# A routed mixture of experts: other queues, places and order for the loads of its sums, and an earlier read of the ring place

## The reference, cut to what matters

```python
router_scores = jax.nn.sigmoid(t @ Wr)
_, idx = jax.lax.top_k(router_scores + expert_bias[None, :], TOPK)
w = jnp.take_along_axis(router_scores, idx, axis=1)
w = w / jnp.sum(w, axis=-1, keepdims=True)
wfull = jnp.zeros((T, E), jnp.float32).at[jnp.arange(T)[:, None], idx].set(w)
g = jnp.einsum('th,ehi->tei', t, Wg)
u = jnp.einsum('th,ehi->tei', t, Wu)
act = jax.nn.silu(g) * u
moe = jnp.einsum('tei,te,eih->th', act, wfull, Wd)
shared = jax.nn.silu(t @ Wsg) * (t @ Wsu) @ Wsd
return resid + (moe + shared).reshape(B, S, H)
```

## Time and profile before

| what | value |
|---|---|
| median of 3 runs | 2467.36 us (2466.81 to 2470.5) |
| the profiled execution | 2468.82 us, span 2467.0 us |
| mean granted TensorE clock | 0.954 |
| PE busy | 2212.2 us, 90% |
| DVE busy | 1313.1 us, 53% |
| ACT busy | 927.0 us, 38% |
| POOL busy | 986.5 us, 40% |
| DMA | 194.38 MB, mean 79 GB/s |

### The profile page before, as it was taken

How to read it: one execution, slowest core, us unless ns; L and a number is a source line. 1 busy time by engine, 2 the same in 40 slices (tenths; PEclk the granted TensorE clock), 3 DMA queues, 4 the chain that set the end, 5 groups by cost and what they waited for, 6 DMA issues and landing times. The chain is left out here.

```text
span 2467.0 us, 41046 instructions
## 1 busy us (share of the span) xinstructions
PE 2212.2 (90%) x15152; PEld 1594.1 (65%) x15152; DVE 1313.1 (53%) x2358; ACT 927.0 (38%) x1630; POOL 986.5 (40%) x787
## 2 busy tenths in 40 slices
PE   7889999688999998889999998578879999979998
PEld 7658776577888887543333333166657777759997
DVE  4563666647777777533333332485762666653333
ACT  1332222344454553245655555013543323232221
POOL 2334544555656563225656564153433101012220
PEclk9999999799999999989999999788999999979999
DMA  3011100221111110657666868630011000011110
GB/s 122 24 58 49 39 27 1 73 82 56 53 60 51 61 43 1 232 169 183 128 127 166 230 163 274 136 88 25 2 55 58 26 26 26 1 52 52 51 51 30
DMA packets 56910, 194.38 MB, mean 79 GB/s; under 512 B 8261, under 2 KB 8517, under 8 KB 49861
## 3 DMA queue, kind: packets, MB, share of 16 engines
q1 hardware_dynamic: 39444, 152.95, 18.6%
q0 software_dynamic: 17280, 38.94, 8.2%
HBM read 158.70 MB, written 33.16 MB: 78 GB/s over the span
## 5 line engine op out<-in xcount | busy, mean ns | idle before, releaser
L2095 PE MATMUL bank<-m_ring,m_bT 128*64 x576 | 265.1, 603 | 22.2 <-issue 13.0
L2097 PE MATMUL bank<-m_upper,m_bT 128*64 128x512 f32 x576 | 265.4, 604 | 0.0
L2008 DVE SCALAR_TENSOR_TENSOR m_prod<-bank,m_slot_rows,m_silu 64x256 f32<-64x256 f32 x144 | 69.6, 483 | 293.5 <-ACT m_silu L1768 291.7
L2095 PEld LDWEIGHTS bank<-m_ring,m_bT 128*64 128x64 f32 x576 | 73.6, 138 | 162.8 <-issue 162.8
L1739 POOL DMA_INDIRECT m_sum<-m_yb,m_idx x72 | 102.8, 1428 | 168.9 <-DVE m_yb L2019 161.1
L1823 ACT ACTIVATE m_upper<-m_ring 128x1024 f32 x144 | 143.5, 1046 | 1.4 <-issue 1.2
L856 ACT ACTIVATE y_att_p_rows<-bank,y_att_n_top 112x375 f32<-112x375 f32 x128 | 71.7, 573 | 189.6 <-DVE y_att_n_top L898 189.6
L2124 PE MATMUL bank<-m_ring,m_aT 128*64 x288 | 135.4, 592 | 0.8 <-DVE m_aT L2025 0.8
L2126 PE MATMUL bank<-m_upper,m_aT 128*64 128x512 f32 x288 | 135.4, 592 | 0.0
L225 PE MATMUL bank<-f_hT_hi,f_w_hi 128*128 128x448 f32 x288 | 109.3, 380 | 9.1 <-PEq L91 2.7
L1283 POOL TENSOR_TENSOR f_att_turned<-f_att_turned,consts 128x448 f32<-128x448 f32 x64 | 74.8, 1170 | 102.7 <-ACT f_att_turned L1333 102.7
(11 more groups left out here) (498 smaller groups left out, 6204.2 us busy)
## 6 DMA issues: line engine op xcount, KB each, us to landing
m_ring<-in_m_w SPq DMA_DIRECT2D x32, 1536.0 KB, 7.7
f_raw<-in_f_wq SPq DMA_DIRECT2D x64, 256.0 KB, 2.6
z_raw<-in_z_w SPq DMA_DIRECT2D x7, 1536.0 KB, 6.4
f_att_wo_raw<-in_f_wo SPq DMA_DIRECT2D x16, 512.0 KB, 3.7
m_sum<-m_slot_rows SPq DMA_DIRECT2D x4, 2048.0 KB, 18.2
x_c_raw<-in_ctxT SPq DMA_DIRECT2D x8, 752.0 KB, 4.3
y_c_raw<-in_ctxT SPq DMA_DIRECT2D x8, 752.0 KB, 4.2
a_raw<-in_a_wqk SPq DMA_DIRECT2D x8, 256.0 KB, 2.6
```

Of the source, the lines that this page charges most:

```text
L2095: pe.matmul(ps_gu[u % 2][0:HP, :], bT[:, n % 2, k, 0:HP], ring[:, bass.ds(slot + at, D)], start=(k == 0), stop=(k == KC - 1))
L2097: o = pe.matmul(ps_gu[u % 2][HP:P, :], bT[:, n % 2, k, HP:P], upper[:, n % 2, at:at + D], start=(k == 0), stop=(k == KC - 1))
```

## The change

Four things are done. SP's loop over the odd sums goes; ACT issues these two loads (`load_odd`), behind its work for block 64 (NBLK - TAIL + 2), and the loads no longer wait for the ring. `add_odd` runs behind the last three blocks, three sequences behind block 69, three behind 70, two behind 71. For the last sums SP issues the four loads of sum 0 into `y`, each with a semaphore of its own, and ACT issues the four of sum 1 into `x2`, between the silu and the copy of shared unit 6; DVE takes the products of units 5, 6 and 7 and the sum of unit 5 ahead of the adds. And PE reads the rank of block n + 1 and works out its place and its count for the ring between the gate products of block n and the down products of block n - 1.

```diff
--- before.py
+++ after.py
@@ -1643,7 +1643,7 @@
 
         (consts_in, wr_in, shared_in, ring_in, rows_set, tail_set, share_set, sums_set) = map(sem, (
             "consts_in", "wr_in", "shared_in", "ring_in", "rows_set", "tail_set", "share_set", "sums_set"))
-        early_in = sem("early_in")
+        early_in = [sem(f"early_in{h}") for h in range(B // 2)]
         late_in = [sem(f"late_in{h}") for h in range(B // 2)]
         rows_in = [sem(f"rows_in{i}") for i in range(NR)]
         summed = [sem(f"summed{i}") for i in range(4)]
@@ -1671,6 +1671,13 @@
         def pairs_in(at, n):
 
             return sum(sums_of(m) == at for m in range(n))
+
+        def load_even(e, i, into, arrived):
+            e.wait_ge(summed[i], 16 * pairs_in(0, NBLK))
+            for h in range(B // 2):
+                e.dma_start(into[:, 2 * h:2 * h + 2, :],
+                            sums_dram[i][2 * h * S:2 * (h + 1) * S, :].rearrange("(b s) d -> s b d", b=2)
+                            ).then_inc(arrived[h], 16)
 
         def unit_of(b):
 
@@ -1707,18 +1714,8 @@
                     sp.wait_ge(dn_done, last + FRONT)
                 sp.dma_start(ring[:, bass.ds(at, EW)], w_dram[bass.ds(expert, 1)].squeeze(0)).then_inc(ring_in, 16)
             sp.wait_ge(ring_in, 16 * E_MOE)
-            for i, into in ((2, y), (3, x2)):
-                sp.wait_ge(summed[i], 16 * pairs_in(i // 2, NBLK))
-                sp.wait_ge(x_done, B)
-                sp.dma_start(into[:, :, :], sums_dram[i][0:T, :].rearrange("(b s) d -> s b d", b=B)).then_inc(odd_in, 16)
-            for i, into in ((0, y), (1, x2)):
-                sp.wait_ge(summed[i], 16 * pairs_in(0, NBLK))
-                if i == 0:
-                    sp.wait_ge(odd_done, B)
-                for h in range(B // 2):
-                    sp.dma_start(into[:, 2 * h:2 * h + 2, :],
-                                 sums_dram[i][2 * h * S:2 * (h + 1) * S, :].rearrange("(b s) d -> s b d", b=2)
-                                 ).then_inc(late_in[h] if i == 1 else early_in, 16)
+            sp.wait_ge(odd_done, B)
+            load_even(sp, 0, y, [early_in[h] for h in range(B // 2)])
 
         @block.gpsimd
         def _(pool):
@@ -1829,6 +1826,12 @@
                 act.activation(upper[:, n % 2, 2 * KC * EI:EW], ring[:, bass.ds(slot + 2 * KC * EI, NC * D)],
                                ACT.Copy).then_inc(upper_done, 1)
 
+            def load_odd():
+                act.wait_ge(x_done, B)
+                for i, into in ((2, y), (3, x2)):
+                    act.wait_ge(summed[i], 16 * pairs_in(1, NBLK))
+                    act.dma_start(into[:, :, :], sums_dram[i][0:T, :].rearrange("(b s) d -> s b d", b=B)).then_inc(odd_in, 16)
+
             collect_rows(0)
             collect_rows(1)
             act.wait_ge(tabs_done, 4)
@@ -1845,9 +1848,16 @@
                     copy_upper_down(n + 1, slot)
                 if n + 2 < NBLK:
                     collect_rows(n + 2)
-            for b in range(FRONT, B):
-                silu_of(unit_of(b))
-                collect_a(unit_of(b))
+                if n == NBLK - TAIL + 2:
+                    load_odd()
+            silu_of(unit_of(FRONT))
+            collect_a(unit_of(FRONT))
+            silu_of(unit_of(FRONT + 1))
+            act.wait_ge(odd_done, B)
+            load_even(act, 1, x2, late_in)
+            collect_a(unit_of(FRONT + 1))
+            silu_of(unit_of(FRONT + 2))
+            collect_a(unit_of(FRONT + 2))
 
         @block.vector
         def _(dve):
@@ -2039,12 +2049,12 @@
                 if n:
                     collect_y(n - 1)
                 collect_block(n)
-                if n >= NBLK - 4:
-                    for b in range(2 * (n - NBLK + 4), 2 * (n - NBLK + 4) + 2):
+                if n >= NBLK - 3:
+                    for b in range(3 * (n - NBLK + 3), min(3 * (n - NBLK + 3) + 3, B)):
                         add_odd(b)
             def add_first(b):
                 dve.wait_ge(add_done, b + 1)
-                dve.wait_ge(odd_done, b + 1)
+                dve.wait_ge(early_in[b // 2], 16)
                 dve.tensor_tensor(x[:, b, :], x[:, b, :], y[:, b, :], ALU.add).then_inc(first_sum, 1)
 
             def add_last(b):
@@ -2056,24 +2066,19 @@
 
             collect_y(NBLK - 1)
             prod_shared(5)
-            dve.wait_ge(early_in, 16 * (B // 2))
-            for b in range(FRONT):
+            prod_shared(6)
+            add_shared(5)
+            prod_shared(7)
+            for b in range(6):
                 add_first(b)
-            add_shared(5)
-            prod_shared(6)
-            add_first(5)
-            for b in range(3):
+            add_shared(6)
+            for b in range(4):
                 add_last(b)
-            prod_shared(7)
-            add_last(3)
-            add_shared(6)
+            add_shared(7)
             add_first(6)
-            add_last(4)
-            add_last(5)
-            add_shared(7)
             add_first(7)
-            add_last(6)
-            add_last(7)
+            for b in range(4, B):
+                add_last(b)
 
         @block.tensor
         def _(pe):
@@ -2224,18 +2229,23 @@
             pe.wait_ge(etab_done, 1)
             turn_rows(0)
             turn_rows(1)
+            def slot_of(n):
+                rank = pe.value_load(rtab[0:1, 2 * n:2 * n + 1], min_val=0, max_val=E_MOE - 1)
+                return pe.snap(rank % RING * EW), pe.snap(rank * 16 + 16)
+
+            slot, loaded = slot_of(0)
             for n in range(NBLK):
-                rank_now = pe.value_load(rtab[0:1, 2 * n:2 * n + 1], min_val=0, max_val=E_MOE - 1)
-                slot = pe.snap(rank_now % RING * EW)
-                pe.wait_ge(ring_in, rank_now * 16 + 16)
+                pe.wait_ge(ring_in, loaded)
                 pe.wait_ge(bT_done, n + 1)
                 gate_up_halves(n, slot)
+                if n + 1 < NBLK:
+                    slot_next, loaded = slot_of(n + 1)
                 if n:
                     down_halves(n - 1, slot_before)
                 if n + 2 < NBLK:
                     turn_rows(n + 2)
                 turn_a(FRONT + n)
-                slot_before = slot
+                slot_before, slot = slot, slot_next
             down_halves(NBLK - 1, slot_before)
             shared_up(FRONT)
             for b in range(FRONT, B):
```

## The result

The changed kernel takes 2428.15 us (median of 4 runs, 2420.88 to 2430.01) against 2468.93 us for the kernel before beside it (4 runs, 2466.81 to 2473.66): a ratio of 0.9825, 95% interval 0.9805 to 0.9845. That is faster, clear of no change though by less than 2%, and 2429.0 was forecast. Its profiled execution took 2430.01 us, with a span of 2428.2 us (before 2467.0). The total came out right, but two terms of its sum did not, and they nearly cancel.

A forecast was written before the change was run, and what follows sets the result against it. PE bound the late loop, with a 26.6 us wait for DVE, itself held by late odd loads. Stage end 1534.3 + 40.1 + 0.3 = 1574.7 against 1612.96: 38.3 us less, so 2429.0 us, range 2414 to 2444.

The forecast's parts named there:

- Part 1: PE's joint between blocks: reading the ring place earlier gains 0.3 us a block, 18 us up to gate 61.
- Rival B: PE's joint keeps its length, since a change of product form costs what the read did: 2448 us, chance 0.12.
- Rival C: PE's register read waits until queued gate products are done, 1.0 us more a block: 2518 us, chance 0.03.
- Part 2: Late loop: ACT issues odd loads early, adds from block 69; a 12 us stall replaces the 27, gate 71 at 1534.3.
- whatever POOL issues meanwhile lands behind them: Late loop: gathers and scatters issued after the odd loads wait for them, a new stall of 12 us.
- they land at about 1499: Late loop: the odd loads, 3.6 MB, take 14 us of all DMA engines after the ring load landing at 1485.
- a 12 us stall in front of gate 67: PE wants block 68's gather at 1492.4, but it lands at 1504 to 1504.5.
- Rival A: Late loop: odd loads do not block the gathers, so the 12 us stall goes: 2417 us, chance 0.2.
- Three adds a block: DVE's late-loop odd adds: six operations, 4.1 us, make the next product 0.4 us late; 0.3 charged once.
- a sign of being wrong: Gather after the odd loads landing within 5 us, blocks staying at 6.4 us, or DVE waiting for pieces behind the loop.
- Part 3: Behind the loop: DVE makes products before adds, ending 40.1 us behind gate 71; gain 2.1 us, second queue 0.2 of issue.

The follow-up runs named there:

- e7: The changed kernel with PE's read of the ring rank and its arithmetic done four times in a row instead of once; 2430.42 us, ratio 0.9839.
- e1: The kernel before with only PE's register read moved behind the gate products; 2444.91 us, ratio 0.9891.
- e4: The changed kernel with 21 ring loads in place of 32, leaving out ranks 21 to 31 that no block reads; 2421.47 us, ratio 0.9804.
- e6: The changed kernel with two odd adds behind each of blocks 68 to 71, as before the change; 2424.03 us, ratio 0.9814.
- e10: The changed kernel with ring loads ended behind the last rank in use and two odd adds behind each of blocks 68 to 71; 2415.12 us, ratio 0.9797.
- e12: The changed kernel itself, same text, run once more; 2429.49 us, ratio 0.9845.
- e9: The changed kernel with SP's ring loads ended behind the last rank that a block reads, by a count from the rank table; 2415.94 us, ratio 0.9791.
- e3: The changed kernel with both last sums issued by SP and DVE's adds in the order of before; 2431.94 us, ratio 0.9835.
- e5: The changed kernel with SP issuing all eight pieces of the last sums and ACT none, DVE's new order kept; 2428.16 us, ratio 0.9844.

## Why the prediction was right, step by step

| term | forecast | profiled execution | off by |
|---|---|---|---|
| gate 1 to gate 61 against before | -18.2 | -19.1 | -0.9 |
| gates 61 to 71 | 77.8 (-18.2) | 73.56 (-22.5) | -4.2 |
| gate 71 to the end | 40.4 (-1.8) | 42.65 (+0.4) | +2.2 |
| gate 1, unchanged code | 0 | +2.6 | +2.6 |
| end of the stage | -38.3 | -38.5 | -0.2 |

The forecast puts gate 61 at 1456.5, though its own 18 us from 1474.7 make 1456.7; the table keeps what it used.

**Part 1 was right, in mechanism and size.** Blocks of 6.11 us, no idle time at the gates, 0.32 us a block against 0.3. The switch from transposes to gate products costs what was taken: the last transpose starts 0.20 us before the gate, 0.11 us between transposes. The read is at the gate (0.1 us behind it, not 0.5), earlier than said. Rival B (the joint keeps its length) and Rival C (the read waits for queued products) fall with this and with e7.

**Part 2: the step that failed** is "whatever POOL issues meanwhile lands behind them", with "they land at about 1499" beside it. The loads were issued when I said (1482.88, forecast 1481.8), but landed at 1503.1 and 1517.6. I had given them all DMA engines for 14 us; they share them with the ring loads, three of which took 10.1, 12.9 and 9.2 us where 7.7 was the step before. And small transfers were not held until the odd loads were in: they landed 0.7 us ahead of to 3.4 us behind the ring load in flight, near what the earlier trace rows had. The gather for block 68, for which I forecast a 12 us stall in front of gate 67, was in time. The stall was 6.5 us, in front of gate 69, with 1.3 and 0.7 before it: 8.5 in place of 12 and the pace of landings behind it. By e1, ring loads at the pace of part 1 make 7.1 us of such waits without any odd load, a cost that the forecast did not have by itself. Rival A, by which the odd loads hold nothing back, was nearer for e4's first scatter, but it charged nothing, and the runs lie between: such a transfer takes 3.6 us alone, 7.2 to 8.9 just behind a ring load, 6.9 and 8.4 beside the odd loads (e4), and up to 11.5 beside both. The Trainium skill (DMA: Bandwidth & Descriptors, Queues, rings and completion order) says that each DMA engine goes round between its queues, packet by packet. The trace agrees in that the scatter of 1482.93 landed 12.7 us before an odd load issued ahead of it, and not in that slipping in would be free.

I had also left out what the clock adds to a stall. PE was busy for 1.49 us of the 8 from 1508 to 1516; from 1516 to 1519 it worked without a pause at a granted clock of 0.50 (1.2 GHz), and from 1522 on at 1.00 (2.4 GHz), as the windows above show. At the half clock the pairs of gate products start 0.85 us apart and not 0.43, and gate 69 to gate 70 took 8.47 us, 2.4 over the usual.

Three adds a block made the product of block 70 late: PE waited 1.1 us for it, and gate 71 came 6.91 us behind gate 70, against 5.74 with two adds (e6, e10; block 70 turns no rows, so it is shorter than 6.11). That is 1.2 us where 0.3 was charged. The other two of PE's three waits for products lie behind gate 71.

The size of this term is not known as closely as the table looks: e12 has 79.05 for the same stretch, and 77.8 lies between the two. What failed is how it comes about, more than its sum.

**Part 3: DVE's order did what was forecast, but the pieces came later.** The forecast put the first piece of sum 0 at 14.45 us behind gate 71, as before; it was at 18.02. That is the second step that failed: each lower scatter waits for the landing of the last one, the ring loads held that chain until 1536.4, which is now 4.7 us behind gate 71, and gate 71 had moved ahead of the chain. Where the unused loads are gone the piece leaves at 14.80 to 15.59 (e10, e9, e4), which bears this out. The 3.6 us cost the end only part of themselves, since product 7 comes no sooner: DVE's six first adds started 23.84 us behind gate 71, where the forecast has 23.3 and its 0.3. From there it took 18.81 us, of which 1.97 are waits for later pieces and 16.84 the work, forecast at 16.8. I had named waits of DVE for pieces behind the loop as a sign of being wrong, and 0.95 and 1.02 us came. With the piece on time e10 ends 39.78 us behind gate 71, close to the 40.1 forecast for this order; the old order has 42.21 with the piece at 14.45. That is 2.4 us for part 3, as forecast (2.1). With late pieces it is worth more: against e3, which has late scatters with the old order, about 4 us. Of this the second queue has nothing, as forecast (e5).

That the total hit to 1 us is thus partly luck: in the profiled execution 4.2 us too pessimistic in the loop, 2.2 too optimistic behind it, and 2.6 in code that nobody changed. Each of these is within what one more execution can move; the mechanism of part 1, the end of the hole and the order of size of what follows it are what the runs bear out.

## What to carry to other kernels

A wait that ends with a load queued behind other loads is cured by issuing the load earlier, here from another queue, but the bytes then compete with everything in flight: price it by the sum of the bytes over the same engines, look at the small transfers that must return in one step of the loop, and ask first whether all of those bytes are needed (here leaving out the unused ring loads was worth 12 us). When the end of a loop moves forward, a chain with a pace of its own, such as accumulating scatters that wait for each other, does not move with it; place what follows it by the chain and not by the loop. A register read belongs where its queue has work ahead.

## What the runs showed of the hardware

- Two 1.8 MB loads took 9.9 and 16.1 us alone, 10.9 and 17.7 beside small transfers, and 20.2 and 34.3 beside ring loads of 1.5 MB (changed kernel), which took 6.9 to 10.1 us without them (before, changed) and then as much as 12.9. The same text once more had 24.7 and 36.0 (e12).
- Small indirect transfers issued in the changed kernel between the odd loads' issue and the landing of the second landed from 0.7 us ahead of to 3.4 us behind the ring load in flight, and up to 12.7 us before an odd load issued ahead of them (a scatter of 1482.93 at 1490.4, the odd load of 1482.88 at 1503.1). They took 3.6 us alone, 7.2 to 8.9 when issued 0.8 us behind a ring load (changed, 13 scatters), 6.9 and 8.4 beside the odd loads (e4), and 7.5 to 11.5 beside both (changed).
- Outside the changed stage the same code took from 1861.4 to 1871.9 us in thirteen profiled executions, so that a gain of under 5 us has to be read in its stage; and in the stage the same text took 558.6 and 566.8 us.
- Behind a wait of 6.51 us PE worked at a granted clock of 0.50 (1.2 GHz), with pairs of gate products 0.85 us apart, and from 1522 us on at 1.00 (2.4 GHz), with 0.43 (changed kernel).
